# Attention and a mixture of experts on one core: another order of steady batches, and a hand-over to the experts rebuilt on it

## What is computed

```python
x = layernorm(x + attn(x))            # 16 heads of 8, causal, softmax(q k^T / sqrt(128)) v, then Wo
logits = x @ gate_w.T                 # 14 experts
top2_p, top2_i = top_k(softmax(logits), 2)
w = top2_p / max(top2_p.sum(-1), 1e-10)
hh = gelu(einsum('nd,edf->nef', x, w1) + b1)      # F = 256
all_out = einsum('nef,efd->ned', hh, w2) + b2
moe = w[:, 0:1] * all_out[n, top2_i[:, 0]] + w[:, 1:2] * all_out[n, top2_i[:, 1]]
x = layernorm(x + clip(x + moe, -100, 100))
```

## Time and profile before

| what | us |
|---|---|
| median of three runs (lowest, highest) | 519.73 (518.69, 521.35) |
| the profiled execution | 516.23 |
| its span, first to last instruction | 514.4 |
| batches 1 to 7 begin (exp of their first bank) | 60.0, 97.1, 135.9, 174.9, 213.0, 251.6, 289.8 |
| batch 7: groups 1, 2, 3 begin; last exp ends | 299.3, 310.2, 318.5; 337.6 |
| first bias addition of a tile; last tile | 342.3; 481.1 |

### The profile page before, as it was taken

The page is one execution under the profiler, slowest core; times in us unless marked ns, Lnnn a source line. Parts: engine busy times, 40 slices in busy tenths (PEclk is TensorE's granted clock), DMA queues, the critical chain, the costliest instruction groups (busy, mean ns, idle before and its releaser), DMA issues.

```text
span 514.4 us, 20509 instructions
## 1 busy us (share of the span) xinstructions
PE 423.7 (82%) x8282; PEld 289.4 (56%) x8282; DVE 341.3 (66%) x907; ACT 324.9 (63%) x777; POOL 289.8 (56%) x495
## 2 busy tenths in 40 slices
PE   7697997999999999999989997487477777788891
PEld 2354464564564565564565453156477666678791
DVE  7986788688589589589589676157644453544286
ACT  5284876777777777777767658245356575656335
POOL 6031434666666666666666777415755656565542
PEclk9999999999999999999999999789668898887997
DMA  6644574564564565553543301131334323226234
GB/s 190 191 137 122 144 208 142 176 183 136 182 184 138 165 194 145 165 164 97 170 134 84 116 29 54 37 91 57 96 107 114 82 77 87 77 71 226 64 110 123
DMA packets 77662, 65.19 MB, mean 127 GB/s; under 512 B 12391, under 2 KB 72046, under 8 KB 77569
## 3 DMA queue, kind: packets, MB, share of 16 engines
q1 hardware_dynamic: 72624, 55.27, 37.7%
q0 software_dynamic: 4512, 8.54, 4.9%
q10 hardware_dynamic: 432, 0.07, 0.1%
HBM read 36.88 MB, written 25.46 MB: 121 GB/s over the span
## 4 chain that ended last, share of the span: by engine, by line
PE 58%; ACT 11%; DVE 10%; issue 8%; another core or an unknown queue 7%; SPq 3%; DMA 2%; POOL 1%; DVEq 0%; ACTq 0%; POOLq 0%
PE psum L1040 18%; PE psum L1127 12%; PE psum L1283 7%; ACT probs L894 7%; PE psum L1074 6%; PE psum L1300 6%; DVE nmax L1448 4%; PE psum L1355 2%; PE psum L1087 1%; PE psum L1275 1%; PE psum L1347 1%; SPq L485 1%; DVE probs L1683 1%; DVE ov L1457 1%
## 5 line engine op out<-in xcount | busy, mean ns | idle before, releaser
L894 ACT ACTIVATE probs<-psum 128x512 f32<-128x512 f32 x320 | 178.1, 598 | 95.0 <-PE psum L1040 78.7
L1448 DVE TENSOR_REDUCE nmax<-psum 128x2 f32<-128x1024 f32 (+7 forms) x256 | 180.6, 743 | 58.9 <-PE psum L1087 41.6
L1040 PE MATMUL psum<-qst,kst 128*32 128x512 bf16 (+3 forms) x2048 | 127.6, 303 | 23.1 <-ACT probs L894 11.6
L778 POOL TENSOR_SCALAR_AFFINE_SELECT probs<-probs 128x512 f32<-128x512 f32 x186 | 85.2, 486 | 56.9 <-ACT probs L894 56.7
L857 POOL DMA_INDIRECT o_dram<-probs,xs x77 | 77.3, 1004 | 67.1 <-DVE probs L1683 42.4
L1074 PE MATMUL psum<-kst,qst 128*32 128x480 bf16 (+15 forms) x2048 | 106.9, 279 | 8.8 <-DVE nmax L1448 4.0
L1127 PE MATMUL psum<-probs,vst 128*32 128x512 f32 (+3 forms) x1024 | 92.6, 439 | 1.1 <-issue 0.7
L1074 PEld LDWEIGHTS psum<-kst,qst 128*32 128x32 bf16 x2048 | 59.4, 96 | 41.7 <-issue 22.7
L1040 PEld LDWEIGHTS psum<-qst,kst 128*32 128x32 bf16 x2048 | 46.6, 96 | 58.5 <-ACT probs L894 39.4
L1087 PE MATMUL psum<-bmask,bident 128*32 128x64 bf16 (+2 forms) x1280 | 73.7, 198 | 0.0
L1087 PEld LDWEIGHTS psum<-bmask,bident 128*32 128x32 bf16 x1280 | 41.8, 97 | 12.4 <-issue 1.1
(11 more groups left out here) (240 smaller groups left out, 659.8 us busy)
## 6 DMA issues: line engine op xcount, KB each, us to landing
kst<-dk SPq DMA_DIRECT2D x62, 128.0 KB
qst<-dq SPq DMA_DIRECT2D x31, 256.0 KB
xs<-xs_dram SPq DMA_DIRECT2D x77, 66.0 KB
dk<-side SPq DMA_DIRECT2D x7, 384.0 KB, 3.3
dq<-side SPq DMA_DIRECT2D x7, 384.0 KB
dk<-side SPq DMA_DIRECT2D x9, 256.0 KB, 3.0
side<-in_xT SPq DMA_DIRECT2D x8, 256.0 KB
dq<-side SPq DMA_DIRECT2D x8, 256.0 KB, 2.4
```

The source lines that it names most:

```text
L778: pool.affine_select(out=view, in_=view, compare_op=ALU.is_ge, fill=0.0, base=0, pattern=[[0, view.shape[1]], [1, P]], channel_multiplier= ...
L894: act.activation(probs[:, c % 2, p, kk * T:(kk + 1) * T], ps_t[:, k % 2, :], ACT.Exp, scale=SCALE).then_inc(S["exp_done"], 1)
L1040: last = pe.matmul(out[32 * g:32 * g + 32], stationary[:, 32 * g:32 * g + 32], moving, skip_group_check=True, **flags)
L1448: last = dve.tensor_reduce(nmax[:, c, 2 * t:2 * t + 2], ps[:, :, at:at + TWO * (t + 1)], AX.X, ALU.max, negate=True)
```

## The change

Each batch gets a plan of its own for the shared bank and what hangs on it: `OPENING` (batch 0), `STEADY`, `TURNING` (6), `CLOSING` (7) and `ENDING` (b = 8). In the steady plan `pv` goes in four places (k = 3, 5, 7, 9), its first piece halved; `normalise` moves from the end of an even group to the start of the next odd group; the turn of rows moves from (1, 1) to (1, 4), "woa" from (1, 3) to (1, 6), "wob" from (1, 5) to (1, 8); ranks are formed a batch later ("rk_late"); rows are normalised one at a time in group 3. The scatters of a steady batch stand at new places, in three pairs and two singles. In batch 7 the first tile table is made in 15 parts over groups 0 and 1 and turned and taken in group 2; the tiles are loaded and four tiles' weights are copied in group 3; PE masks groups 2 and 3, whose scores go round four banks (`LATE_BANKS`); `add_bias` of batch 7 is POOL's; a copy of batch 6's rows moves from ACT to DVE. The first 13 steps are laid out anew, `OUT_FIRST` is 7, the weights have ten places, y has three banks, and the second table is turned at tile 15 and taken at 18.

```diff
-        MISC = {
-            (0, 2): "q", (0, 9): "va",
-            (1, 1): "vb", (1, 3): "woa", (1, 5): "wob",
-            (2, 4): "rk", (3, 2): "k"}
-        PART_STEP = 2
+        PART_STEP = 3
-        PV_AT = {4: (0,), 8: (1, 3, 2)}
-        PV_LAST = {6: (0,), 9: (1, 3, 2)}
+        PIECES = {"0a": (0, 0, T // 2), "0b": (0, T // 2, T), "1": (1, P, T), "3": (3, 3 * P, T), "2": (2, 2 * P, T)}
+        PV_AT = {3: ("0a",), 5: ("0b",), 7: ("1",), 9: ("3", "2")}
+        PV_LAST = {1: ("0a", "0b"), 3: ("1", "3", "2")}
-        OT_AT = (0, 8, -1)
-        ON_AT = (1, 1)
+        OT_AT = (1, 0, -2)
+        STEADY = {
+            "misc": {(0, 1): "q", (0, 9): "va", (1, 1): "vb", (1, 3): "rk_late", (1, 6): "woa", (1, 8): "wob", (2, 1): "k"},
+            "on": (1, 4),
...
+        CLOSING = {
+            "misc": {(0, 9): "va", (1, 1): "vb", (1, 7): "woa", (2, 0): "wob", (2, 6): "rk"},
+            "on": (1, 4),
+            "shared": {(1, 8): "woa", (2, 1): "wob", (2, 7): "rk"},
+            "stats": {(1, 9): (0, 1), (2, 1): (2, 3)}, "aggr": (2, 1),
+            "top": {(2, 1): (0,), (2, 2): (1,), (2, 3): (2,), (2, 4): (3,)}, "top_late": {},
+            "ln": {(2, 4): (0, 1), (2, 5): (2, 3)}, "copy": (2, 7), "rank": (2, 7)}
...
         LAST = {
-            "scatter": {(0, 0): (2,), (0, 1): (3, 4), (1, 0): (5, 6), (1, 1): (7,)},
+            "scatter": {(0, 0): (0,), (0, 1): (1, 2), (1, 0): (3, 4), (1, 1): (5, 6), (2, 0): (7,)},
             "early": {(2, 1): range(TOPK * NQ)}}
-        TABLE_AT = ((2, 0), (3, 0), (3, 7), (3, 8))
+        TABLE_PARTS = {(0, 2): 0, (0, 4): 1, (0, 6): 2, (0, 8): 3, (1, 0): 4, (1, 2): 5, (1, 3): 6, (1, 4): 7, (1, 5): 8,
+                       (1, 6): 9, (1, 7): 10, (1, 8): 11, (3, 4): 12, (3, 6): 13, (3, 8): 14}
+        TABLE_TURNED, TABLE_TAKEN = (2, 3), (2, 4)
-        SCATTER_NEXT = {(3, 1): (0, 1)}
-        SCATTER_AT = {(0, 0): (2,), (0, 1): (3,), (1, 0): (4,), (1, 1): (5,), (2, 0): (6,), (2, 1): (7,)}
+        SCATTER_AT = {(1, 1): (0,), (2, 0): (1, 2), (2, 1): (3,), (3, 0): (4, 5), (3, 1): (6, 7)}
+        MASKED_FROM = 2
+        LATE_BANKS = (4, 5, 2, 3, 4, 5, 2, 3, 4, 5, 2, 3, 4, 5, 2, 3, 4, 5, 4, 5)
+        def masked_by_pe(b, c):
+            return closing(b) and c >= MASKED_FROM
+        def km_bank(b, c, k):
+            return LATE_BANKS[(c - (NG - 2)) * NBANK + k] if wide(b, c) else 4 + k % 2
-        OUT_AHEAD = 4
-        OUT_FIRST = 9
+        OUT_AHEAD = 5
+        OUT_FIRST = 7
...
-                            for upto, view in () if last_group(b, c) else (
+                            for upto, view in () if masked_by_pe(b, c) else (
...
+                            if closing(b) and (c, p) == (2, 1):
+                                add_bias(b)
                             if closing(b) and (c, p) in LAST["early"]:
                                 send(b - 1, 1 - odd, LAST["early"][c, p])
...
-                    if c == 0 and b == B:
+                    if c == 3 and closing(b):
                         sp.wait_ge(S["tables_ready"], 1)
...
                         load_tiles(0, STEP)
...
+                        if closing(b) and (c, k) == plan(b)["copy"]:
...
+                            dve.tensor_copy(x1s[1 - odd][1][:, :, 0:D], x1s[1 - odd][0][:, :, 0:D]
+                                            ).then_inc(S["x1b_ready"], 1)
```

More of the change, by code:

```diff
@@ new lines, in first @@
+            def first(j):
+                pe.wait_ge(S["xsT_copied"], j + 1)
+                pe.wait_ge(S["w_copied"], j + 1)
+                if j >= 2:
+                    pe.wait_ge(S["gelu_done"], j - 1)
+                else:
+                    pe.wait_ge(S["exp_done"], NBANK * NG * B - 4)
+                for ch in range(FC):
+                    last = pe.matmul(psum[:, 2 + j % 2, P * ch:P * ch + P], expert(j)[:, P * ch:P * ch + P],
+                                     xsT[:, j % RING, :], start=True, stop=True)
+                last.then_inc(S["h_filled"], 1)
@@ new lines, in second @@
+            def second(j):
+                pe.wait_ge(S["gelu_done"], j + 1)
+                if y_free(j):
+                    pe.wait_ge(S["y_copied"], y_free(j))
+                elif j < 2:
+                    pe.wait_ge(S["exp_done"], NBANK * NG * B)
+                elif y_home(j) == 6:
+                    pe.wait_ge(drained["ot"], NG * B // 2)
+                else:
+                    pe.wait_ge(S["tables_ready"], 2)
+                for ch in range(FC):
+                    last = pe.matmul(y_bank(j), hT_sb[:, j % RING, P * ch:P * ch + P],
+                                     expert(j)[:, W2_AT + P * ch:W2_AT + P * ch + D],
+                                     start=(ch == 0), stop=(ch == FC - 1))
+                last.then_inc(S["y_filled"], 1)
@@ L1648, in second_table @@
+                if part == 14:
+                    link(dve.scalar_tensor_tensor(out=region[:], in0=jumps[:, 0, :], scalar=float(REG), in1=region[:],
+                                                  op0=ALU.mult, op1=ALU.add))
             def second_table():
@@ L1771, in body @@
-                        if closing(b) and (c, k) == TABLE_AT[0]:
-                            first_table(0)
-                        if (c, k) == RANK_AT and live(b - 1) and b >= B - 1:
+                        if (c, k) in plan(b)["top_late"] and live(b - 2):
+                            for part in plan(b)["top_late"][c, k]:
+                                top_part(b - 2, part)
+                        if b == B and (c, k) in LATE_LOOKS:
+                            look(LATE_LOOKS[c, k])
+                        if b == B:
+                            for what, j in TAIL_DVE.get((c, k), ()):
+                                if what == "weights":
+                                    weights(j)
+                                else:
+                                    add(j)
```

461 lines of the change are left out of this document (253 added, 208 removed).

## The result

The changed kernel takes 515.02 us (median of 20 runs, 512.03 to 518.60) beside 518.72 for the kernel before (20 runs, 515.50 to 523.77): a ratio of 0.9929, 95% interval 0.9906 to 0.9951, so 0.7% or 3.7 us faster. The prediction was 512.8 within 503 to 524, which is 0.987 of the kernel before. The profiled execution fell from 516.23 to 512.03 us (the lowest of the 20 runs), the span from 514.4 to 510.3.

What follows compares the result with a forecast made beforehand. Steady batches were taken as bound by PE, with POOL's indirect transfers delaying handoffs. Steady -0.9, batch 7 -4 and tiles -2 sum to -6.9, from 516.23 to 509.3 profiled, times 1.0068 gives 512.8 us, range 503 to 524.

Steps and rivals of the forecast that it cites:

- POOL's transfers hold up what waits for PE: Whole kernel: while POOL runs an indirect transfer, other engines learn late what PE has finished; back-to-back transfers add up.
- Scatters, +3.7: Batches 1 to 6: more pairs at 1.3 us, fewer singles at 0.4; +3.7 us, bounds -1.2 and +15.7.
- The rival with the whole 2.63: Pairs cost their whole 2.63 us hold-up, scatters 15.7 instead of 3.7; time 524.8 us; chance 0.17.
- Output projection, -3.6: Six steady batches: projections three banks later cover PE's 0.79 us wait for turned rows; -3.6 us, bounds -4.7 and 0.
- The steady sum: Steady batches: scatters 3.7, output projection -3.6, pieces of `pv` and copies -1.0; together -0.9 us.
- Batch 7, -4: Groups 2 and 3: burst starts where it did, four banks shorten the exps behind it; -4 us, bounds -12.1 and +2.
- at nothing together: Batch 7, groups 0 and 1: table parts onto DVE, statistics out; cost nothing, or 1 us if idle time doesn't cover it.
- Tiles, -2: Tiles after attention: batch 7's burst starts after seven outputs instead of nine; -2 us, bounds -5 and 0.
- signs of being wrong: Listed signs: batch period moves over 1 us, exps run through the burst, slow scatters, batch 7's burst not waiting for outputs.
- four banks carry the exps through: Batch 7, rival: four banks carry ACT's exps through the burst; 504.6 us; chance 0.13.
- the burst only moves: Rival: eight scatters still stand together, so batch 7 and the tiles give nothing; 518.8 us; chance 0.15.
- The copies of weights do not hold POOL's transfers: Judges the rival for batch 7 that DVE's copies hold POOL's transfers, burst ending 2.6 us later; 515.4 us; chance 0.05.

Runs made afterwards that it cites:

- x1: Changed kernel with eight more indirect transfers, a pair in each group of batch 1; batch 1 takes 38.64 us instead of 34.59.
- y4: Kernel before with only the two output projections, and what hangs on them, two banks later in batches 1 to 6; ratio 1.0115 to the kernel before.
- z1: Changed kernel with one POOL operation of about 0.66 us between the two scatters of each pair; ratio 0.9789 to the kernel before.
- w1: Kernel before with POOL spacing operations in pairs, between scatters of batches 6 and 7 and behind output transfers; ratio 0.9650 to the kernel before.
- x4: Changed kernel with batch 7's four row normalisations and their copy together on ACT, earlier; ratio 0.9890 to the kernel before.
- x2: Changed kernel with five POOL operations of its own, no transfers, in each group of batch 1; batch 1 takes 35.53 us instead of 34.59.

## Why the prediction came out as it did

The direction and the range held, and so did the reading that POOL's transfers hold up what waits for PE. The size was half of what was forecast, and that the sign came out owes something to luck. Of the -6.9 forecast, -6 was to come from batch 7 and the tiles; in the profile these together gave +0.5. The gain came from batches 0 to 2 (-2.8) and from stretches that were put at little or nothing.

*Scatters, +3.7.* The price of 1.3 us a pair is of the right size: a pair in batch 1 cost 1.0 (x1), and taking 18 pairs apart gained 7 us, 0.4 each, where 1.3 - 0.8 = 0.5 was to be had. The price of a single was not tested. The rival with the whole 2.63 is out; in the changed kernel batch 4's pairs show idle times of 2.54 and 2.10, and its groups 0 and 2 are only 1.6 us longer than those of batch 1, which has no scatters.

*Output projection, -3.6.* The size was right (-0.8 a group in y4, -1.3 in the changed kernel with its scatters gone), but a cover was not named: `reciprocal_spread` had to move too, or the step costs 1.9 us in the next group, as in y4. PE's idle time before the projections is 2.5 us in all instead of 5.5:

```profile
L1099 PE MATMUL psum<-wo_sb,onT_sb 128*32 128x142 f32 x256 | 12.8, 286 | 2.5 <-DVE onT_sb L1554 2.0 <-issue 0.5
```

The steady sum was -0.9 and came out at -3.7. Its -0.9 in batches 3 to 6 is no gain: seven other profiles of this code took 153.8 to 154.8 us there, and the kernel before 153.86. By the prediction's own prices these four batches were to lose about 0.2 us each, so that fits. The gain lies before them. Batch 2 takes 36.73 us instead of 38.77, 2.1 of it in its group 0, which has no pair now; that was in the count. Batch 1 takes 34.59 instead of 37.11, and this is no chance (34.2 to 34.9 in all profiles of the code); it has no scatters in either kernel, and the projection and the pieces were to give it only some 0.8. Batch 0 takes 37.1 to 38.3 us in the changed code and took 36.39. No run explains these two.

*Batch 7, -4.* It gave -0.8. Groups 2 and 3 gave -2.1: the tail behind the burst was nearly right (5.0 us against 4.4), its start was not, 10.3 us into group 2 instead of 8.9. The rows were normalised 7.3 us into it, at 314.99, as worked out, and the copy and `add_bias`, taken as 1.6 together, ended after 1.55. The step that failed is what stood behind them, put at nothing. DVE's timeline:

```profile
315.02 1.52 DVE L1883 COPY x_even_second<-x_even_first 128x512 f32<-128x512 f32 x1
```

The copy ran until 316.54, beside POOL's `add_bias`, 314.96 to 316.26 (its row is above), and only then came DVE's three operations for the positions, which ended at 317.23, and the burst at 318.05. These last 1.5 us were not counted.

Groups 0 and 1, costed "at nothing together", took 1.3 more. Their windows in the changed kernel (columns as in the earlier trace rows):

```profile
286.07:296.47 10.40, 8.76 (x236) 5.11 (x232) 7.90 (x16) 6.00 (x12) 7.80 (x13) 1.00 0.35 99
296.47:307.72 11.25, 9.34 (x252) 6.04 (x248) 10.21 (x30) 6.13 (x14) 6.83 (x10) 1.00 0.10 28
```

Group 0 took 9.54 us before, so 0.9 of the loss is there, where DVE is idle for 2.5 us; taking the pairs apart changes nothing in it (10.45 in z1), and its cause stays open. Group 1 lost 0.4. DVE is busy 10.21 us in it, which looks as if the table's parts did not fit; but with the same parts and the pairs apart it takes 9.39 (z1), so what made it long is the hold-up of its pairs, worth 1.9 here and 0.7 in the order of before (10.86 against 10.18 in w1).

*Tiles, -2.* They came out at +1.3 in this profile and at about nothing in the mean of the seven that share the code (143.2 against 143.45). The burst of batch 7 started 23.7 us behind the last exp, not 19.5. That it waited for something other than the outputs is one of the prediction's own signs of being wrong. The last output ended at 353.28, and POOL waited 3.56 us for ACT's copy of the rows, which stood behind a step of a tile; the copy was not looked up:

```profile
355.31 0.63 ACT L1011 ACTIVATE x_odd_second<-x_odd_first 128x512 f32<-128x512 f32 x1
```

The positions too were late: DVE had them at 354.32, 21.2 us behind the last exp, where the 19.5 of before had been taken over. In x4, with the copy early, POOL waits for them (1.80 us), and the burst starts 21.4 behind.

*The rivals.* That four banks carry the exps through is out (one exp in 10 us). That the burst only moves is wrong for groups 2 and 3, which gained 2.1, but its sum, nothing from batch 7 and the tiles, was nearer to what these stretches gave than the forecast's -6. The copies of weights do not hold POOL's transfers: in the changed kernel four of them ran from 319.09 to 321.28, and the scatters at 319.44 and 320.75 took 1.00 and 0.97 us.

Two slips bear on none of this: 9 x 1.1 is 9.9 and not 9.5, and the batch period of before was 38.5 us in batches 3 to 6, not 38.8.

## What to carry to other kernels

When engines idle on a releaser that the profile can't name, look at what another engine does at the same time; here every such wait, in all 13 profiles, ended within 2.1 us behind the end of an indirect transfer of POOL's (among the tiles, where one comes about every 1.6 us, that alone says little). Keep these transfers apart: here half to one microsecond of anything else between two of them, even useless work, was cheaper than the hold-up of everything that waits for PE. And when a step is moved to spare one engine's wait, look at what is queued behind the other engines that consume it.

## What the runs showed of the hardware

Beside indirect transfers 0.3 us apart (0.97 us each), engines that wait for PE mostly start only behind the last of them. Behind a burst of eight the next exp started 0.1 to 1.5 us after its end, and one or two exps passed between its first transfer and its last, in all nine profiles that have it together. PE itself starts its products there one or two at a time, 0.7 us apart, while DVE's copies of weights, which do not wait for PE, run on beside the same transfers (319.09 to 321.28). With gaps of 0.8 us the ten exps took 7.2 us instead of 16.2; operations of POOL's of more length than the pair of transfers do not have this effect (x2). Whether PE's semaphore writes wait, or something else holds both PE and the engines that wait for it, no run shows; that stays open.

The copy of 128x512 float32 took 1.52 us on DVE beside an addition of POOL's that had started 0.06 us earlier, and ended 0.28 us behind it; on ACT the same copy takes 0.63. In z1 the copy started first, and there the addition is the longer one, 1.44 us instead of 1.30:

```profile
307.72 0.43 DVE L1896 COPY x_even_second<-x_even_first 128x512 f32<-128x512 f32 x1 [1.91 <-ACT x_even_first L1001]
```

```profile
307.86 1.44 POOL L880 TENSOR_TENSOR xbo<-xb,bo_bc 128x568 f32<-128x568 f32 x1
```

The Trainium skill, "SBUF — State Buffer", section "SBUF: two separate sides", has a rule for this: DVE, in some operations, and POOL share a port as a lock, and whoever starts first keeps the other waiting. The trace agrees with it here, in both orders. The case which that section warns of, DVE's copies of float32 that starve POOL's transfers, did not show: scatters beside copies of weights took 0.97 and 1.00 us.
